# Experts in pairs: two gate-and-ups, two downs and eight transpositions in a row on TensorE

## The chip, the cores and the metric

The kernel runs on one core of a Trainium2 chip as one program. The metric is the device time of one execution in microseconds (us). The core has five engines, each with its own instruction queue: TensorE (PE, with its weight loads as PEld), VectorE (DVE), ScalarE (ACT), GpSimd (POOL) and SyncE (SP). They meet only at semaphores.
## The reference

Two transformer layers over 2048 tokens of 256 columns, float32. Layer 0 is attention and a dense feed-forward. Layer 1 is attention over groups of four and a mixture of 64 experts, of which each token takes 8. The change touches only the experts, with what the kernel does beside them:

```
_route:  scores = sigmoid(x @ gate_weight.T);  topk_idx, topk_w  (8 experts of a token)
for each expert e:
    inter = silu(x @ wg.T) * (x @ wu.T)          # 256 -> 176
    out  += (inter @ wd.T) * w_full[:, e]        # 176 -> 256
x = x + attention(xn) + moe(xn)
```

## The kernel before

The tokens' 16,384 choices are sorted by expert and cut in segments of 64 rows. Two segments, which may belong to two experts, make a block of 128 rows; there are 160 blocks (NBLK). A block goes through these steps, each named by its function:

- GpSimd gathers the block's rows from memory (`gather`, L189) into one of 8 slots of x.
- TensorE transposes them (`transpose_x`, L1832, two 128x128 transpositions into ps_xT), VectorE copies the result to xT (`copy_x`, L1719).
- TensorE multiplies with gate and up (`gate_up`, L1845). The first 64 rows use the weights of the first segment's expert where they were loaded; the other 64 use a copy of the second segment's expert, s_gu, made by ScalarE (`copy_gate_up`, L1671). So each step is two matmuls, each on 64 of the array's columns, that start together. In the trace there are four such steps per block, since each float32 product is done in two passes.
- ScalarE takes silu of the gate half (`silu`, L1653), VectorE multiplies with the up half (`gate`, L1736).
- TensorE transposes the product h (`transpose_h`, L1857, two transpositions into ps_hT), VectorE copies it to hT (`copy_h`, L1744).
- TensorE multiplies with down (`down`, L1868, again four steps of two), ScalarE scales by the router's weight (`copy_y`, L1662) and GpSimd scatters the rows to memory (`store`, L1634). The router's weight is picked by VectorE (`weigh`, L1727). The second expert's down weights are copied by ScalarE too (`copy_down`, L1676).

All 160 blocks are written out in Python: the order of each engine is the order of its code, and each step waits for semaphores that count the blocks done (`gu_ready`, `h_ready`, `hT_copied` and so on). TensorE's turn for block j is gate and up of j, down of j - 2, the register with the expert's number for j + 1 (L1837), the transpositions of x of j + 2, and those of h of j - 1. VectorE fits layer 1's attention (`attention`, L1757 to L1784) between the blocks, one step of it per block, 40 blocks to each of four batches; one exponential per batch is ScalarE's (L1691). GpSimd's turn is one gather and one scatter. SyncE loads the experts' weights, 16 experts deep (L1582 and L183 on).

After the last block TensorE multiplies the attention result with its output weights (L1897, L1904), SyncE reads the scattered rows back (L1615), and TensorE and VectorE add them up (L1930, L1547).

Of the kernel before, what the change touches and what calls it, by code (L numbers as in the profile page):

```python
# [18 lines left out]
ACT = mybir.ActivationFunctionType  # L19
AX = mybir.AxisListType  # L20

P = 128
B, T, D = 4, 512, 256
# [3 lines left out]
KD = D // P  # L27
# [22 lines left out]
HI1 = INTER1 // 2  # L50
# [1424 lines left out]
def layer1_experts(nc, t, ident, late, ring, x_sb, qkv1, seg_expert, expert_f, inv, dst, last, latest):  # L1475
# [3 lines left out]
    with ctx:  # L1479
        NS, NW, NY, NQ = ring.NS, ring.NW, SCATTERS, 4  # L1480
        LEAD, BEHIND, NF = 2, 3, 5
# [4 lines left out]
        xT = sbuf(ctx, nc, "e_xT", [P, 2, KD * P])  # L1486
# [4 lines left out]
        hT = sbuf(ctx, nc, "e_hT", [HI1, 2, 2 * P])  # L1491
# [9 lines left out]
        yT = sbuf(ctx, nc, "e_yT", [P, 2, KD, P])  # L1501
# [4 lines left out]
        ps_y = psum(ctx, nc, "e_ps_y", [P, 512])  # L1506
# [52 lines left out]
        def gate_up_copied(j):  # L1559

            return j + 1 if j < 2 else 2 * j - 1

        def down_copied(j):

            return 2 * j + 4 if j + 2 < NBLK else NBLK + j + 1
# [53 lines left out]
        def _(pool):  # L1619
# [9 lines left out]
            for j in range(NS, NS + LEAD):  # L1629
                refill(j)  # L1630
# [15 lines left out]
        def _(act):  # L1646
# [9 lines left out]
            def copy_y(j):  # L1656
                act.wait_ge(y_ready, j + 1)
                act.wait_ge(weighed, j + 1)
                if j >= NY:

                    act.wait_ge(y_out[j % NY], j // NY * 16)
                nc.scalar.activation(y[:, j % NY, :], ps_y[:, 0:D], ACT.Copy,  # L1662
                                     scale=weight[:, j % NQ:j % NQ + 1]).then_inc(y_copied, 1)
# [19 lines left out]
            for j in range(NBLK + 2):  # L1683
                n, l, k = part(j) if j < NBLK else (0, 0, None)
                if j + 2 < NBLK:
                    experts.append(expert_of(j + 2))
                if j < NBLK:
                    silu(j)
                if k == 5:
                    act.wait_ge(s_ready, n * B + B)  # L1690
                    nc.scalar.activation(e1[:, :, :], s1[:, :, :], ACT.Exp,  # L1691
                                         scale=SCALE1).then_inc(e_ready, 1)
                if j >= 2:
                    copy_y(j - 2)
                if j + 2 < NBLK:
                    copy_gate_up(j + 2, experts[j + 2])
                if j < NBLK:
                    copy_down(j, experts[j])
# [14 lines left out]
        def _(dve):  # L1713
# [3 lines left out]
            def copy_x(j):  # L1717
                dve.wait_ge(xT_ready, j + 1)
                V.tensor_copy(xT[:, j % 2, :], ps_xT[:, 0:D]).then_inc(xT_copied, 1)  # L1719
# [19 lines left out]
            def copy_h(j):  # L1739
                dve.wait_ge(hT_ready, j + 1)  # L1740
                if j >= 2:

                    dve.wait_ge(y_ready, j - 1)
                V.tensor_copy(hT[:, j % 2, :], ps_hT[0:HI1, 0:2 * P]).then_inc(hT_copied, 1)  # L1744
# [46 lines left out]

            copy_x(0)
            copy_x(1)
            weigh(0)
            for j in range(NBLK + 1):
                if j < NBLK:
                    gate(j)
                if j + 1 < NBLK:
                    weigh(j + 1)
                if j + 2 < NBLK:  # L1800
                    copy_x(j + 2)
                if j >= 1:
                    copy_h(j - 1)
                if j < NBLK:
                    attention(*part(j))
# [20 lines left out]
        def _(pe):  # L1826
            def transpose_x(j):
                pe.wait_ge(x_in[j % NS], (j // NS + 1) * 16)
                if j:
                    pe.wait_ge(xT_copied, j)  # L1830
                for k in range(KD):
                    ins = nc.tensor.transpose(ps_xT[:, k * P:(k + 1) * P],  # L1832
# [6 lines left out]
            def gate_up(j, expert):  # L1839

                pe.wait_ge(xT_copied, j + 1)
                pe.wait_ge(w_copied, gate_up_copied(j))
                for k in range(KD):
                    for r, w in ((0, w_gu[:, bass.ds(expert & (NW - 1), 1), k, :]), (1, s_gu[:, j % 2, k:k + 1, :])):
                        ins = nc.tensor.matmul(  # L1845
                            ps_gu[r * SEG:(r + 1) * SEG, j % 2, 0:2 * INTER1],
                            xT[:, j % 2, k * P + r * SEG:k * P + (r + 1) * SEG],
# [4 lines left out]
            def transpose_h(j):  # L1852
                pe.wait_ge(h_ready, j + 1)
                if j:
                    pe.wait_ge(hT_copied, j)
                for k in range(2):
                    ins = nc.tensor.transpose(ps_hT[0:HI1, k * P:(k + 1) * P],  # L1857
# [3 lines left out]
            def down(j, expert):  # L1861
                pe.wait_ge(hT_copied, j + 1)
                pe.wait_ge(w_copied, down_copied(j))
                if j:
                    pe.wait_ge(y_copied, j)
                for k in range(2):
                    for r, w in ((0, w_d[0:HI1, bass.ds(expert & (NW - 1), 1), k, :]), (1, s_d[:, j % 2, k:k + 1, :])):
                        ins = nc.tensor.matmul(  # L1868
                            ps_y[r * SEG:(r + 1) * SEG, 0:D], hT[:, j % 2, k * P + r * SEG:k * P + (r + 1) * SEG],
# [4 lines left out]
            transpose_x(0)  # L1874
            transpose_x(1)
            now, before, oldest = expert_of(0), None, None
            for j in range(NBLK + 2):
                after = None
                if j < NBLK:
                    gate_up(j, now)  # L1880
                if j >= 2:
                    down(j - 2, oldest)
                if j + 1 < NBLK:
                    after = expert_of(j + 1)
                if j + 2 < NBLK:
# [141 lines left out]
```

## Time and profile before

| | |
|---|---|
| median of 3 runs | 1199.44 us (1199.24 to 1202.48) |
| the profiled execution, its own time | 1196.38 us |
| its span (first to last instruction) | 1194.2 us |
| TensorE, matmuls | 1109.2 us busy, 93% |
| VectorE, ScalarE, GpSimd | 715.6, 658.9, 464.1 us busy |
| gate and up matmuls (L1845) | 2 x 640, 476 ns each |
| down matmuls (L1868) | 2 x 640, 380 ns each |

The experts' stage is the last big one, from about 679 us to 1138 us of the span. The busy time of TensorE counts each matmul from its start to its modelled end; matmuls overlap, so a step's real cost is the distance from its start to the next start. An average of busy time over the whole span says little about this stage; the rows below are of this stage alone.

### The profile page before, as it was taken

What the parts mean: (1) busy time and instruction counts of PE and PEld (TensorE: products, weight loads), DVE (VectorE), ACT (ScalarE), POOL (GpSimd) and SP (SyncE); (2) the same over time, 40 slices, a digit from 0 to 9 for tenths busy, and PEclk for the clock granted to TensorE, in tenths of its full rate; (3) what the DMA queues carried; (4) which work ended last, traced back from release to release, by engine and by line L of the source; (5) the groups of instructions that cost most, each with busy time, mean ns of one, the idle gap of its engine ahead of it and who ended that gap; (6) DMA issues with size and microseconds to landing.
All of it is one profiled execution on the core that took longest, in us unless ns stands there. A gap on an engine that the chain in (4) does not pass through costs nothing. (4 is left out here: it accounts for less than half of the span.)

```text
span 1194.2 us, 25537 instructions
## 1 busy us (share of the span) xinstructions
PE 1109.2 (93%) x7606; PEld 655.3 (55%) x7606; DVE 715.6 (60%) x2605; ACT 658.9 (55%) x1340; POOL 464.1 (39%) x525
## 2 busy tenths in 40 slices
PE   6679999999999999997888699999999999999985
PEld 3355666666666666654655454555455555545564
DVE  6486666565666666641259665566565656566556
ACT  4214454555555545455335567777777777777620
POOL 4332222223131000000310266777677767777500
PEclk9899999999999999999989799999999999999997
DMA  7400131113111201001104483764648436766267
GB/s 242 89 10 18 24 51 30 31 30 52 30 31 30 51 21 23 21 16 45 49 24 123 114 228 123 222 192 124 194 141 258 157 119 187 226 186 213 76 252 289
DMA packets 81682, 129.68 MB, mean 109 GB/s; under 512 B 32776, under 2 KB 53001, under 8 KB 81034
## 3 DMA queue, kind: packets, MB, share of 16 engines
q1 hardware_dynamic: 61576, 76.94, 22.7%
q0 software_dynamic: 15360, 47.21, 12.8%
q10 hardware_dynamic: 4616, 3.91, 1.1%
q8 instruction: 68, 1.11, 0.4%
q14 instruction: 62, 0.51, 0.1%
HBM read 97.57 MB, written 30.05 MB: 107 GB/s over the span
## 5 line engine op out<-in xcount | busy, mean ns | idle before, releaser
L684 DVE CUSTOM_DVE_ANT_0 a_masked<-a_ps_s,a_mask 128x512 bf16<-128x512 f32 (+3 forms) x512 | 229.9, 487 | 157.9 <-PE a_ps_s L843 154.1
L600 ACT ACTIVATE a_probs<-a_ps_e 128x512 f32<-128x512 f32 (+1 forms) x384 | 188.2, 527 | 119.9 <-PE a_ps_e L863 118.9
L1845 PE MATMUL e_ps_gu<-e_w_gu,e_xT 128*64 x640 | 226.3, 476 | 1.0 <-ACT e_s_gu L1671 1.0
L1845 PE MATMUL e_ps_gu<-e_s_gu,e_xT 128*64 128x352 f32 x640 | 226.3, 476 | 0.0
L189 POOL DMA_INDIRECT yn<-rows,inv x160 | 156.5, 978 | 138.4 <-DVE inv L1404 60.8
L1634 POOL DMA_INDIRECT y<-e_y,dst x160 | 172.3, 1077 | 59.3 <-issue 43.0
L1868 PE MATMUL e_ps_y<-e_w_d,e_hT 88*64 x640 | 165.0, 380 | 5.0 <-DVE e_hT L1744 5.0
L1868 PE MATMUL e_ps_y<-e_s_d,e_hT 88*64 88x256 f32 x640 | 165.1, 380 | 0.0
L860 PE MATMUL a_ps_e<-a_qT,a_kT 75*128 75x512 bf16 (+3 forms) x512 | 140.8, 303 | 2.1 <-ACT a_probs L600 1.8
L843 PE MATMUL a_ps_s<-a_kT,a_qT 72*128 72x512 bf16 (+3 forms) x512 | 131.3, 300 | 11.5 <-DVE a_headmax L684 11.3
L1736 DVE TENSOR_TENSOR e_h<-e_sg,e_ps_gu 128x176 f32<-128x176 f32 x160 | 53.9, 337 | 134.2 <-ACT e_sg L1653 112.0
L919 PE MATMUL a_ps_f<-a_xnT,a_w_gu 128*128 128x256 f32 x512 | 125.5, 388 | 5.6 <-DVE a_hT L709 3.2
L1868 PEld LDWEIGHTS e_ps_y<-e_w_d,e_hT 88*64 88x64 f32 x640 | 86.5, 136 | 79.2 <-issue 55.1
L1671 ACT ACTIVATE e_s_gu<-e_w_gu 128x704 f32 x160 | 124.8, 781 | 3.5 <-SPq L1582 3.5
L1662 ACT ACTIVATE e_y<-e_ps_y,e_weight 128x256 f32<-128x256 f32 x160 | 75.8, 474 | 85.7 <-PE e_ps_y L1868 85.7
L1845 PEld LDWEIGHTS e_ps_gu<-e_w_gu,e_xT 128*64 128x64 f32 x640 | 75.1, 137 | 81.0 <-issue 81.0
L863 PE MATMUL a_ps_e<-a_causal,a_identb 128*128 128x128 bf16 x512 | 112.4, 220 | 0.0
L456 POOL CAST a_m_parts<-a_negmaxT 32x128 bf16<-32x128 f32 x16 | 4.5, 281 | 275.4 <-DVE a_negmaxT L727 155.0
L919 PEld LDWEIGHTS a_ps_f<-a_xnT,a_w_gu 128*128 128x128 f32 x512 | 93.6, 192 | 22.8 <-DVE a_hT L709 10.8
L1719 DVE COPY e_xT<-e_ps_xT 128x256 f32<-128x256 f32 x160 | 67.9, 424 | 52.7 <-PE e_ps_xT L1832 52.5
L1676 ACT ACTIVATE e_s_d<-e_w_d 88x512 f32 x160 | 98.7, 617 | 0.0
L860 PEld LDWEIGHTS a_ps_e<-a_qT,a_kT 75*128 75x128 bf16 x512 | 49.2, 97 | 75.1 <-ACT a_probs L600 67.3
(243 smaller groups left out, 1893.1 us busy)
## 6 DMA issues: line engine op xcount, KB each, us to landing
e_w_gu<-e_gu SPq DMA_DIRECT2D x64, 352.0 KB
e_w_d<-e_down SPq DMA_DIRECT2D x64, 176.0 KB
a_qT<-qk_parts SPq DMA_DIRECT2D x48, 192.0 KB
e_w_gu<-y SPq DMA_DIRECT2D x12, 768.0 KB, 6.3
qk_parts<-a_stage SPq DMA_DIRECT2D x16, 256.0 KB, 2.6
e_w_gu<-y SPq DMA_DIRECT2D x4, 1024.0 KB, 7.0
qkv<-y SPq DMA_DIRECT2D x12, 256.0 KB
yn<-rows,inv POOLq DMA_INDIRECT x160
```

The source lines that it names most:

```text
L189: eng.indirect_dma_start(self.x[:, j % self.NS, :], None, t["rows"], bass.IndirectOffsetOnAxis(inv[:, j:j + 1], 0)).then_inc(self.x_in[j % ...
L600: nc.scalar.activation(probs[:, i % HKV, UCOL[u]:UCOL[u + 1]], ps_e[:, (i * 3 + u) % 2, 0:w], ACT.Exp, scale=SCALE0).then_inc(exp_done, 1)
L684: ins = V.tensor_tensor_reduce(masked[:, n % 2, c:c + w], ps_s[:, n % 2, c:c + w], mask[:, T - w:T], 1.0, -3e38, ALU.add, ALU.max, headmax ...
L843: ins = nc.tensor.matmul(ps_s[:, x % 2, c:c + (a + 1) * P], qT[0:MROW, n % NQ, g, a * P:(a + 1) * P], kT[0:MROW, b % 2, g, 0:(a + 1) * P], ...
L860: nc.tensor.matmul(ps_e[:, x % 2, c:c + T - a * P], kT[:, b % 2, g, a * P:(a + 1) * P], qT[:, n % NQ, g, a * P:T], start=True, stop=False, ...
L863: ins = nc.tensor.matmul(ps_e[:, x % 2, c:c + P], identb[:, :], causal[:, :], start=False, stop=True, skip_group_check=True)
L919: ins = nc.tensor.matmul(ps_f[:, w * HALF:(w + 1) * HALF], w_gu[:, k, w, i * P:(i + 1) * P], xnT[:, n % NX, k, :], start=(k == 0), stop=(k ...
L1634: pool.indirect_dma_start(t["y8"], bass.IndirectOffsetOnAxis(dst[:, j:j + 1], 0), y[:, j % NY, :], None).then_inc(y_out[j % NY], 16)
L1671: nc.scalar.activation(s_gu[:, j % 2].rearrange("p k i -> p (k i)"), w_gu[:, bass.ds(expert & (NW - 1), 1), :, :].rearrange("p a k i -> p ...
L1676: nc.scalar.activation(s_d[:, j % 2].rearrange("p k d -> p (k d)"), w_d[0:HI1, bass.ds(expert & (NW - 1), 1), :, :].rearrange("p a k d -> ...
L1845: ins = nc.tensor.matmul(ps_gu[r * SEG:(r + 1) * SEG, j % 2, 0:2 * INTER1], xT[:, j % 2, k * P + r * SEG:k * P + (r + 1) * SEG], w.rearran ...
L1868: ins = nc.tensor.matmul(ps_y[r * SEG:(r + 1) * SEG, 0:D], hT[:, j % 2, k * P + r * SEG:k * P + (r + 1) * SEG], w.rearrange("p a d -> p (a ...
```

## The change

TensorE takes two blocks per turn: both gate-and-ups, both downs of the pair before, the two expert numbers of the next pair, the four transpositions of x of the pair after next, and the four of h of this same pair. The transposed x of two blocks fills one bank of ps_xT and the transposed h of two blocks one bank of ps_hT, so `copy_x` and `copy_h` are done once per pair at twice the width (512 columns). ps_y has two banks, one for each block of a pair. xT and hT double, and yT, used after the stage, lies in xT. Before the first gate and up four blocks are transposed, not two. ScalarE, VectorE and GpSimd are put in the matching order; GpSimd's scatters follow four blocks behind, not three, and the router's weights have eight places, not four.

```
-            for j in range(NBLK + 2):
-                after = None
-                if j < NBLK:
-                    gate_up(j, now)
-                if j >= 2:
-                    down(j - 2, oldest)
-                if j + 1 < NBLK:
-                    after = expert_of(j + 1)
-                if j + 2 < NBLK:
-                    transpose_x(j + 2)
-                if 1 <= j <= NBLK:
-                    transpose_h(j - 1)
-                now, before, oldest = after, now, before
+            for j in range(4):
+                transpose_x(j)
+            oldest, now = None, [expert_of(j) for j in range(2)]
+            for m in range(PAIRED + 1):
+                two = (2 * m, 2 * m + 1)
+                if m < PAIRED:
+                    for j in two:
+                        gate_up(j, now[j % 2])
+                if m:
+                    for j in two:
+                        down(j - 2, oldest[j % 2])
+                if m + 1 < PAIRED:
+                    after = [expert_of(j + 2) for j in two]
+                if m + 2 < PAIRED:
+                    for j in two:
+                        transpose_x(j + 4)
+                if m < PAIRED:
+                    for j in two:
+                        transpose_h(j)
+                oldest, now = now, after
...
 (ScalarE, one pair)
+                    for j in two:
+                        silu(j)
+                        if k == 5: ... the exponential
+                        copy_gate_up(j + 2, experts[j + 2])
+                    for j in two:
+                        copy_y(j - 2)
+                    for j in two:
+                        copy_down(j, experts[j])
...
 (VectorE, one pair)
+                gate(j)
+                attention(*part(j))
+                gate(j + 1)
+                attention(*part(j + 1))
+                copy_x(m + 2)
+                copy_h(m)
+                weigh(j + 4)
+                weigh(j + 5)
...
 (GpSimd)
-            for i in range(LEAD, NBLK + BEHIND):
-                if i + NS < NBLK:
+            for i in range(NBLK + BEHIND):
+                if i + NS + LEAD < NBLK:
                     pool.wait_ge(gu_ready, i + 1)
-                    refill(i + NS)
+                    refill(i + NS + LEAD)
                 if i >= BEHIND:
                     store(i - BEHIND)
```

TensorE before, from one block's down to the next gate and up, in the middle of the stage (e_w_gu and e_w_d are the experts' weights, e_s_gu and e_s_d ScalarE's copies):

```order
L1868 MATMUL e_ps_y<-e_w_d,e_hT 64x256
L1868 MATMUL e_ps_y<-e_s_d,e_hT 64x256
L1837 TENSOR_LOAD seg_expert
L1837 ISA x2
L1832 MATMUL e_ps_xT<-ident_sb,yn 128x128 x2
L1857 MATMUL e_ps_hT<-ident_sb,e_h 88x128 x2
L1845 REGISTER_ALU
L1845 ISA
L1845 MATMUL e_ps_gu<-e_w_gu,e_xT 64x352
```

The same place in the changed kernel, where the lines of the code have moved:

```order
L1879 MATMUL e_ps_y<-e_w_d,e_hT 64x256
L1879 MATMUL e_ps_y<-e_s_d,e_hT 64x256
L1845 TENSOR_LOAD seg_expert
L1845 ISA x2
L1845 TENSOR_LOAD seg_expert
L1845 ISA x2
L1840 MATMUL e_ps_xT<-ident_sb,yn 128x128 x4
L1867 MATMUL e_ps_hT<-ident_sb,e_h 88x128 x4
L1854 REGISTER_ALU
L1854 ISA
L1854 MATMUL e_ps_gu<-e_w_gu,e_xT 64x352
```

Two register loads stand together, the transpositions are eight in a row, and this passage comes once in two blocks.

VectorE before, one block of the stage (e_h is gate's product, e_pick is weigh, e_mx and e_s are attention):

```order
L1736 TENSOR_TENSOR e_h<-e_sg,e_ps_gu 128x176
L1727 SCALAR_TENSOR_TENSOR e_pick,e_weight<-l_iota_f,expert_f,yn 128x64
L1719 COPY e_xT<-e_ps_xT 128x256
L1744 COPY e_hT<-e_ps_hT 88x256
L1764 TENSOR_REDUCE e_mx<-e_s 128x16
L1766 TENSOR_TENSOR e_s<-e_s,e_mx 128x16
```

and in the changed kernel, one pair:

```order
L1741 TENSOR_TENSOR e_h<-e_sg,e_ps_gu 128x176
L1762 TENSOR_TENSOR e_prod<-qkv 128x768
L1741 TENSOR_TENSOR e_h<-e_sg,e_ps_gu 128x176
L1765 TENSOR_REDUCE e_s<-e_prod 128x48
L1724 COPY e_xT<-e_ps_xT 128x512
L1749 COPY e_hT<-e_ps_hT 88x512
L1732 SCALAR_TENSOR_TENSOR e_pick,e_weight<-l_iota_f,expert_f,yn 128x64 x2
```

The step of attention now stands right behind each gate product, ahead of the second gate product and of both copies, and weigh stands last.

## Rows read from the trace of the kernel before

**Rows 1.** Stretches: length, busy us (instructions) per engine, clock, DMA share, GB/s
```profile
695.02:1113.00 417.98, 414.10 (x2965) 215.40 (x2966) 251.58 (x881) 305.01 (x606) 304.71 (x297) 1.00 0.58 183
```
**Rows 2.** Waits of TensorE, 692.2 to 1129: us in total, times, longest
```profile
PE e_ps_y L1868 <- DVE e_hT L1744: 3.8, 4, 1.0
```
**Rows 3.** Timeline of TensorE: start, duration, instruction, count
```profile
801.24 0.38 PE L1868 MATMUL e_ps_y<-e_w_d,e_hT 88*64 x1
...
801.55 0.44 PE L1832 MATMUL e_ps_xT<-ident_sb,yn 128*128 128x128 f32 x2
801.83 0.38 PE L1857 MATMUL e_ps_hT<-ident_sb,e_h 128*88 128x128 f32 x2
802.14 0.51 PE L1845 MATMUL e_ps_gu<-e_w_gu,e_xT 128*64 x1
...
802.49 0.46 PE L1845 MATMUL e_ps_gu<-e_w_gu,e_xT 128*64 x1
...
803.37 0.38 PE L1868 MATMUL e_ps_y<-e_w_d,e_hT 88*64 x1
...
804.02 0.38 PE L1868 MATMUL e_ps_y<-e_w_d,e_hT 88*64 x1
...
804.92 0.51 PE L1845 MATMUL e_ps_gu<-e_w_gu,e_xT 128*64 x1
```
**Rows 4.** Line L1857, 801 to 1110 us: duration ns, least/median/most
```profile
L1857 PE MATMUL e_ps_hT<-ident_sb,e_h x220: 272/273/273, 801.8 to 1109.6; 128*88 128x128 f32 x110
```
**Rows 5.** Timeline of ScalarE and VectorE, the same block, [idle before <-releaser]
```profile
802.04 0.78 ACT L1671 ACTIVATE e_s_gu<-e_w_gu 128x704 f32 x1
...
802.37 0.41 DVE L1744 COPY e_hT<-e_ps_hT 88x256 f32<-88x256 f32 x1
...
803.59 0.32 ACT L1653 ACTIVATE e_sg<-e_ps_gu 128x176 f32<-128x176 f32 x1 [0.25 <-PE e_ps_gu L1845]
...
804.00 0.34 DVE L1736 TENSOR_TENSOR e_h<-e_sg,e_ps_gu 128x176 f32<-128x176 f32 x1 [0.89 <-DVE e_s L1760]
```
**Rows 6.** Line L1784, attention's longest step: duration ns, least/median/most
```profile
L1784 DVE TENSOR_REDUCE qkv<-e_prod x16: 405/856/1960, 730.2 to 1118.7; 128x256 f32<-128x256 f32 x4, 128x256 f32<-128x512 f32 x4, 128x256 f32<-128x768 f32 x4, 128x256 f32<-128x1024 f32 x4
```
**Rows 7.** Timeline at the first of the four exponentials
```profile
719.10 1.28 ACT L1691 ACT_TABLE_LOAD   x1
...
720.39 0.34 ACT L1691 ACTIVATE e_e<-e_s 128x160 f32<-128x160 f32 x1
...
725.30 0.42 PE L1868 MATMUL e_ps_y<-e_w_d,e_hT 88*64 x1 [0.95 <-DVE e_hT L1744]
```
**Rows 8.** TensorE's sequencer (PEldq), lines L1837 and L1830: durations ns, first start
```profile
L1837 PEldq TENSOR_LOAD <-seg_expert x109: 298/303/572, 803.1 to 1107.9; - x109
...
L1830 PEldq EVENT_SEMAPHORE  x109: 51/51/51, 803.7 to 1108.6; - x109
```
**Rows 9.** GpSimd's groups, 692 to 1100: busy us, mean ns | idle before
```profile
L1634 POOL DMA_INDIRECT y<-e_y,dst x144 | 155.6, 1080 | 43.9 <-issue 39.0 <-ACT e_y L1662 2.1 <-DVE e_pick L1727 1.2
L189 POOL DMA_INDIRECT yn<-rows,inv x145 | 141.8, 978 | 70.3 <-issue 46.2 <-PE e_ps_gu L1845 16.1 <-PE e_ps_xT L1832 6.4
```
**Rows 10.** Timeline at the start of the stage
```profile
679.74 0.94 POOL L189 DMA_INDIRECT yn<-rows,inv  x1 [2.96 <-POOLq L1158]
...
680.99 0.95 POOL L189 DMA_INDIRECT yn<-rows,inv  x1 [0.30 <-issue]
...
684.95 0.69 PE L1832 MATMUL e_ps_xT<-ident_sb,yn 128*128 128x128 f32 x2 [0.54 <-DMA yn<-rows,inv]
...
689.16 0.80 PE L1845 MATMUL e_ps_gu<-e_w_gu,e_xT 128*64 x1
```
**Rows 11.** Stretches again, the first two blocks
```profile
681.70:689.50 7.80, 7.16 (x24) 2.80 (x26) 2.16 (x10) 3.25 (x7) 5.92 (x7) 0.50 1.15 229
```
**Rows 12.** Timeline at the end of the stage
```profile
1129.28 0.51 PE L1845 MATMUL e_ps_gu<-e_w_gu,e_xT 128*64 x1
...
1138.95 0.97 POOL L1634 DMA_INDIRECT y<-e_y,dst  x1 [1.07 <-ACT e_y L1662]
```

More of the change, by code:

```diff
@@ L1559, in gate_up_copied @@
         def gate_up_copied(j):
-            return j + 1 if j < 2 else 2 * j - 1
+            return j + 1 if j < 2 else 4 * (j // 2) - 2 + j % 2 + 1
         def down_copied(j):
-            return 2 * j + 4 if j + 2 < NBLK else NBLK + j + 1
+            return 4 * (j // 2) + j % 2 + (5 if j + 2 < NBLK else 3)
         def part(j):
@@ L1635, in store @@
                                         y[:, j % NY, :], None).then_inc(y_out[j % NY], 16)
-            for i in range(LEAD, NBLK + BEHIND):
-                if i + NS < NBLK:
+            for j in range(NS, NS + LEAD):
+                refill(j)
+            for i in range(NBLK + BEHIND):
+                if i + NS + LEAD < NBLK:
                     pool.wait_ge(gu_ready, i + 1)
-                    refill(i + NS)
+                    refill(i + NS + LEAD)
                 if i >= BEHIND:
@@ L1790, in add_attention @@
                 V.tensor_tensor(x_sb[:, i, :], x_sb[:, i, :], ps_out[q % 2][:, 0:D], ALU.add).then_inc(o_added, 1)
[L1792 to L1797, printed above, removed]
-                if j + 1 < NBLK:
[L1799 to L1805, printed above, removed]
+            for m in range(2):
+                copy_x(m)
+                for j in (2 * m, 2 * m + 1):
+                    weigh(j)
+            for m in range(PAIRED):
+                j = 2 * m
+                gate(j)
[5 more added lines that the diff above has]
+                copy_h(m)
+                if m + 2 < PAIRED:
+                    weigh(j + 4)
+                    weigh(j + 5)
                 if j == FIRST_ROWS_AT:
@@ L1828, in transpose_x @@
                 pe.wait_ge(x_in[j % NS], (j // NS + 1) * 16)
-                if j:
-                    pe.wait_ge(xT_copied, j)
+                if j >= 2 and j % 2 == 0:
+                    pe.wait_ge(xT_copied, j // 2)
                 for k in range(KD):
-                    ins = nc.tensor.transpose(ps_xT[:, k * P:(k + 1) * P],
+                    c = j % 2 * KD * P + k * P
+                    ins = nc.tensor.transpose(ps_xT[:, c:c + P],
                                               x[:, j % NS, k * P:(k + 1) * P], ident[:, :])
@@ L1853, in transpose_h @@
                 pe.wait_ge(h_ready, j + 1)
-                if j:
-                    pe.wait_ge(hT_copied, j)
+                if j >= 2 and j % 2 == 0:
+                    pe.wait_ge(hT_copied, j // 2)
                 for k in range(2):
-                    ins = nc.tensor.transpose(ps_hT[0:HI1, k * P:(k + 1) * P],
+                    c = j % 2 * 2 * P + k * P
+                    ins = nc.tensor.transpose(ps_hT[0:HI1, c:c + P],
                                               h[:, j % 2, k * HI1:(k + 1) * HI1], ident[:, :])
```

82 lines of the change are left out of this document (39 added, 43 removed).

## The prediction

> **What bounds the kernel now.** I read the table of stretches first. In the experts' stage, about 455 of the 1194 us, TensorE is busy 414.1 of 418.0 us, VectorE 251.6, ScalarE 305.0 and GpSimd 304.7, and the granted clock is 1.00 [rows 1]. The waits come next: over the same stage TensorE waits for another engine only four times, 3.8 us in all, each time for the copy of hT [rows 2]. So the stage lasts as long as TensorE's own row of instructions, and one block of it is the unit of the sum.
>
> The timeline of one block shows where its time goes [rows 3]. Each line is one of two matmuls that start together on the two halves of the array's columns. From one gate-and-up start to the next it is 804.92 - 802.14 = 2.78 us. Inside a group the starts come evenly: gate and up every (803.37 - 802.49)/3 = 0.293 us, down every (804.02 - 803.37)/3 = 0.217 us. A transposition takes 0.109: the two of hT begin at 801.83, the group ends at 802.21 and one lasts 0.273 [rows 3, 4], so the second began at 801.94. Between the groups more goes by:
> - last down to first transposition: 801.55 - 801.24 = 0.31, which is 0.10 over the step of 0.217
> - the first transposition: two steps take 801.83 - 801.55 = 0.28, which is 0.06 over 2 x 0.109
> - last transposition to gate and up: 802.14 - 801.83 = 0.31, which is 0.09 over 2 x 0.109
> - the first gate-and-up step: 802.49 - 802.14 = 0.35, which is 0.06 over 0.293.
> From gate and up to down nothing extra shows. So 0.31 us of each block's 2.78 are the two changes between 64-column matmuls and full-width transpositions.
>
> **The change part by part.** The matmuls, their shapes and their number stay. TensorE's order becomes two gate-and-ups, two downs, four transpositions of x, four of h, so both changes come once per pair.
>
> *Switching.* 78 pairs lie between the third block and the last pair: 78 x 0.31 = 24.2 us saved. A pair takes 2 x 2.78 - 0.31 = 5.26 us. Bounds: if the 0.10 at the entry belongs to something that stays with each block, 78 x 0.21 = 16.4; above 0.31 no row shows anything to gain.
>
> *Transposition of h now follows its own pair.* Before, it waited a whole block; now only the two downs and x's four transpositions cover it. Within a pair from t = 0 at its first gate and up: silu can start 803.59 - 802.14 = 1.45 later, the gate product 804.00 - 802.14 = 1.86 later [rows 5]. The second block's are 1.18 later, at 2.63 and 3.04, h ready at about 3.4. ScalarE does silu (0.32), the copy of the next gate-and-up weights (0.78 from 1.77 to 2.55) and is free for the second silu at 2.63. The transposition that needs the second h comes at 8 x 0.293 + 8 x 0.217 + 0.16 + 6 x 0.109 = 4.9. VectorE can push the second gate product out by the attention step of the even block, 0.41 to 1.96 us by the longest of its steps [rows 6]: at most 2.2 + 1.96 + 0.34 = 4.5. That is still in time. Cost 0; the cover is 1.5 us in most pairs and 0.4 in the worst.
>
> *The copies are twice as wide.* The trace has no 512-wide copy. hT's copy of 256 columns takes 0.41 [rows 5]. The bounds are 0.41 (the width is free) and 0.82 (two copies); I take 0.69, a fixed part of some 0.13 paid once. x's copy starts at 5.0, when its transpositions are through, and hT's ends at 6.4 (5.8 and 6.6 at the bounds). The next pair's down is due at 5.26 + 2.35 = 7.6. Cover 1.2 us, nothing either way. Four pairs hold the longest steps of attention: with 1.96 in the odd block alone the copies still end at 6.8, with as much in the even one at 8.7, 1.1 late. Bound 4 us, taken 0, since the even block's step is a shorter one.
>
> *Exponential.* Its four stalls stay. Two table loads of 1.28 and the exponential (0.34) stand between two silus [rows 7]. Before, that makes the down wait for hT 0.95 [rows 7]. Now the second silu of that pair comes at 1.77 + 1.28 + 0.25 + 0.78 + 1.28 = about 5.4, h at 6.1 against 4.9 due: 1.2 each. Against 0.95 and the slower restart behind it (some 0.25) that is even; bounds -1 to +2 us for the four.
>
> *GpSimd.* One gather and one scatter per block: 0.978 + 1.080 busy and twice the least gap of 0.30 [rows 9] make 2.66 per block, 5.32 a pair, against TensorE's 5.26 and 5.33 with the four stalls spread over the pairs. It is on the edge. But a gather has three pairs (over 15 us less its landing) until TensorE needs it, and a scatter eight slots. In 146 blocks it would fall behind by 146 x 0.03 = 4 us at most, and the last ten blocks need no gather. Cost 0.
>
> *Start.* Now four gathered blocks must be there before the first gate and up; only two were. The third's gather is issued at 679.74 and holds TensorE until 684.95; the fourth's at 680.99 [rows 10], so by the same 5.2 us it lands at 686.2. The clock is at 0.50 (1.2 GHz) in that stretch [rows 11], where everything takes double: 8 gate-and-up steps 4.7 us. First gate and up 686.7, second h ready about 692.5, third block's gate and up 691.9 to 693.3, by whether the clock has risen meanwhile. Before it was at 689.16 [rows 10]. Cost 2.7 to 4.1; I take 3.4. The Trainium skill (TensorE: Matmul & The Clock Gate, Part 4: PE-mode transpose) says that transpositions do not count as TensorE activity for the clock. By it the later end would be right, 0.7 us more; no row here separates it.
>
> *Tail.* From the second-last block's gate and up to the last scatter: 1138.95 - 1129.28 = 9.67 us [rows 12]. Now, by the same steps: gate and up 2.4, down 1.7, four transpositions 0.6, latency and copy 1.0, down to the first y 1.1, ScalarE's copy 0.5, two scatters: the last begins at 8.8. Gain 0.9. The output stage behind it is untouched.
>
> Sum: -24.2 + 3.4 - 0.9 = -21.7 us. The profiled execution took 1196.38 us, so it would be 1174.7. The median of the runs shown is 1199.44, 3.1 above it; the forecast in the terms of those runs is 1177.7.
>
> **The rivals.**
> A, the forecast: the switches go. 1177.7.
>
> B, GpSimd or late gathers take part of it. For it: it has 5.32 of work in 5.33 us, and single scatters take longer. Against it: the slack above. To cost anything its pace must exceed 2.67 + 13/146 = 2.76 us per block; it would then be near 1186 (half of the switches' gain lost, up to 1190).
>
> C, the sequencer is the bound: slower. The place is the two register loads behind two downs. When the load came at 803.1 [rows 8] the array stood at the last gate-and-up step, so all of one down, 8 matmuls and 8 weight loads, had been dispatched. That is all the row shows; two downs behind one gate and up want 48. If only 16 fit, the load starts when the second down starts, 4 x 0.217 = 0.87 before the transpositions, and two loads take 1.2: at least 0.33 late per pair, some 0.4 with what follows them. 79 x 0.4 = 31.6, so 1199.4 + 31.6 - 21.7 = 1209.3. It decides when less than about 28 instructions fit; at 0.27 us per pair the gain is gone.
> The Trainium skill (TensorE: Matmul & The Clock Gate, the table at its head) gives a depth of 64 for the queue. By that figure C would not occur; the rows here only show 16.
>
> D, the 0.31 us is not switching but goes with each block (its waits and register work). Against it: no extra shows between gate and up and down, where the same kind of waits stand. Then only start and tail count: 1199.4 + 2.5 = 1201.9.
>
> E, the clock falls. The eight transpositions and the stall at the exponential leave some 2.4 us with no matmul, four times. At the start a stretch of 7.8 us runs at 0.50 [rows 11] and costs half of it; four of those are 15.6, giving 1193.3. Against it: before, the stalls are followed by no drop (1.00) [rows 1].
> The rule quoted above, that transpositions are no activity, speaks for E; the stage of rows 1 has a switch to them in every block and shows full clock.
>
> **Chances.** A 0.80, B 0.08, C 0.05, D 0.03, E 0.04. A, B and E are faster: 0.91 with the doubt that some of B may end within 0.3%. C and a part of what I haven't thought of are slower: 0.06. D with the rest: 0.03. The bound of 0.3% (3.6 us) is about what a measurement of this kernel can tell from no change. The range: down from 1177.7, the exponential's 1 us, the better start (0.7) and the runs' own spread (3 us) give 1173; up, 16.4 instead of 24.2 gives 1185.5, with the later start and 2 us at the exponential 1188.
>
> **What would show it.** In the profile after, pairs of blocks 5.26 us apart; inside one, 0.31 us between down and transpositions and between these and gate and up once per pair, and the second gate and up right behind the first at 0.29. TensorE's waits list four for h of some 1.2 us and nothing else of size. The third gate and up starts near 692.6. Copies of 512 take about 0.69 us. GpSimd's gaps shrink to 0.30. C would show as 0.7 us instead of 0.31 between down and transpositions, with nobody named for it; B as waits of TensorE for gathered rows or of ScalarE's y copy for scatters; E as a clock below 1.00 between 700 and 1100. I am wrong if a pair takes more than 5.5 us.

## The result and the profile after

| | before | after |
|---|---|---|
| median of the first comparison, us | 1200.96 (4 runs, 1199.24 to 1204.78) | 1183.06 (4 runs, 1178.64 to 1184.52) |
| profiled execution, own time, us | 1196.38 | 1184.52 |
| its span, us | 1194.2 | 1182.7 |

The ratio after over before is 0.9844, with a 95% interval of 0.9813 to 0.9876: 17.9 us faster at the medians, where 21.7 were forecast (1177.7, range 1173 to 1188). On two other chips the sign was the other one, 1.010 and 1.008. The experiments below had to explain that as well. Ratios, here and below, are of fast runs alone; the only slow runs are three of the kernel before on the second chip.

Cut at four events that both traces have, the program reads so, in us:

| part | before | after | difference | forecast |
|---|---|---|---|---|
| span's start to the first transposition of x | 679.14 | 687.59 | +8.45 | 0 |
| to the third block's gate and up | 10.02 | 15.58 | +5.56 | +3.4 |
| to the second-last block's gate and up | 440.12 | 415.46 | -24.66 | -24.2 |
| to the last scatter | 9.67 | 8.90 | -0.77 | -0.9 |

The first row is code that the change doesn't touch. It differs between executions of one kernel too (684.52 and 685.76 in two more profiles of the changed kernel, 682.56 in one more of before, 683.77 in a kernel that is the one before up to there and ran beside the first experiments), and the 679.14 is the earliest of all fourteen profiles. The three rows of the stage sum to -19.9.

**The middle.** The timeline of TensorE in the profile after, one border between pairs; the lines answer to [rows 3]:
```profile
803.18 0.38 PE L1879 MATMUL e_ps_y<-e_w_d,e_hT 88*64 x1
...
803.49 0.66 PE L1840 MATMUL e_ps_xT<-ident_sb,yn 128*128 128x128 f32 x4
803.98 0.60 PE L1867 MATMUL e_ps_hT<-ident_sb,e_h 128*88 128x128 f32 x4
...
806.93 0.38 PE L1879 MATMUL e_ps_y<-e_w_d,e_hT 88*64 x1
...
808.76 0.66 PE L1840 MATMUL e_ps_xT<-ident_sb,yn 128*128 128x128 f32 x4
```
From one group of transpositions to the next it is 808.76 - 803.49 = 5.27 us, where 5.26 were forecast and two blocks took 5.57. The 0.31 between the last down and the first transposition is there as before, once per pair.

The waits of TensorE, 680 to 1120 us, as [rows 2] shows them of before (us in total, times, longest):
```profile
PE e_ps_xT L1840 <- DMA yn<-rows,inv: 6.4, 2, 4.8
PE e_ps_xT L1840 <- PEq L1158: 4.3, 1, 4.3
PE e_ps_hT L1867 <- DVE e_h L1741: 4.1, 4, 1.0
PE e_ps_gu L1854 <- DVE e_xT L1724: 1.1, 1, 1.1
```
Four waits of 1 us for h, at the four exponentials; all the rest stands at the start of the stage. The stretch of the middle part, whose fields are those of [rows 1], the width of x's copy and GpSimd's groups, which answer to [rows 9]:
```profile
703.17:1118.63 415.46, 411.33 (x3118) 236.29 (x3117) 254.77 (x770) 317.34 (x637) 306.85 (x304) 1.00 0.60 187
```
```profile
L1724 DVE COPY e_xT<-e_ps_xT x78: 669/692/693, 703.1 to 1113.5; 128x512 f32<-128x512 f32 x78
```
```profile
L189 POOL DMA_INDIRECT yn<-rows,inv x148 | 150.4, 1016 | 55.8 <-issue 32.5 <-DVE e_pick L1732 11.3 <-PE e_ps_gu L1854 11.0
L1633 POOL DMA_INDIRECT y<-e_y,dst x144 | 145.7, 1012 | 45.5 <-issue 25.0 <-ACT e_y L1663 7.9 <-PE e_ps_gu L1854 7.3
```
The clock is 1.00 (2.4 GHz). The 512-wide copy takes 0.69 us. GpSimd has 101 us of gaps beside 296 of work, so it doesn't set the pace.

**The start.** Timeline, and under it TensorE's sequencer at the lines that read the experts' numbers (durations in ns, first and last start):
```profile
689.43 0.98 POOL L189 DMA_INDIRECT yn<-rows,inv  x1 [0.30 <-issue]
...
695.41 0.69 PE L1840 MATMUL e_ps_xT<-ident_sb,yn 128*128 128x128 f32 x2 [1.54 <-DMA yn<-rows,inv]
...
696.14 0.69 DVE L1724 COPY e_xT<-e_ps_xT 128x512 f32<-128x512 f32 x1 [6.53 <-PE e_ps_xT L1840]
...
697.24 0.84 PE L1854 MATMUL e_ps_gu<-e_w_gu,e_xT 128*64 x1 [1.14 <-DVE e_xT L1724]
```
```profile
L1845 PEldq TENSOR_LOAD <-seg_expert x4: 303/310/487, 695.4 to 698.5; - x4
L1845 PEldq FUSED_REGOPS  x4: 151/154/165, 696.0 to 698.8; - x4
```
The fourth block's transposition begins at 695.41, when its gather has landed, and the first register load begins at the same 695.4. The sequencer had not gone past the transposition that waited. The loads that the prediction counted as free so stand in the open here, beside the copy of x.

### The profile page after: what moved, and what is told of

It reads as the page before. It is cut to its first block and busy times, and to the rows that moved or that the text cites. A ratio compares the mean times of both kernels' runs of the same rounds, so it can differ in the third digit from the quotient of the medians.

```text
span 1182.7 us, 25082 instructions
## 1 busy us (share of the span) xinstructions
PE 1087.1 (92%) x7605; PEld 667.5 (56%) x7606; DVE 704.8 (60%) x2445; ACT 655.8 (55%) x1340; POOL 459.1 (39%) x525
## 5 line engine op out<-in xcount | busy, mean ns | idle before, releaser
L1854 PE MATMUL e_ps_gu<-e_w_gu,e_xT 128*64 x640 | 208.6, 469 | 1.1 <-DVE e_xT L1724 1.1
L189 POOL DMA_INDIRECT yn<-rows,inv x160 | 162.1, 1013 | 122.3 <-DVE inv L1404 60.5
L1854 PE MATMUL e_ps_gu<-e_s_gu,e_xT 128*64 128x352 f32 x640 | 208.6, 469 | 0.0
L1633 POOL DMA_INDIRECT y<-e_y,dst x160 | 161.3, 1008 | 60.5 <-issue 28.9
L1879 PE MATMUL e_ps_y<-e_w_d,e_hT 88*64 x640 | 151.4, 379 | 0.9 <-DVE e_hT L1749 0.9
L1879 PE MATMUL e_ps_y<-e_s_d,e_hT 88*64 88x256 f32 x640 | 151.4, 379 | 0.0
L1854 PEld LDWEIGHTS e_ps_gu<-e_w_gu,e_xT 128*64 128x64 f32 x640 | 81.7, 137 | 90.6 <-issue 90.6
L1724 DVE COPY e_xT<-e_ps_xT 128x512 f32<-128x512 f32 x80 | 55.2, 690 | 92.7 <-PE e_ps_xT L1840 92.6
L1654 ACT ACTIVATE e_sg<-e_ps_gu 128x176 f32<-128x176 f32 x160 | 50.7, 317 | 85.1 <-PE e_ps_gu L1854 79.8
L1677 ACT ACTIVATE e_s_d<-e_w_d 88x512 f32 x160 | 90.9, 617 | 0.0
```

What stands on the lines that cost most here:

```text
L189: eng.indirect_dma_start(self.x[:, j % self.NS, :], None, t["rows"], bass.IndirectOffsetOnAxis(inv[:, j:j + 1], 0)).then_inc(self.x_in[j % ...
L1633: pool.indirect_dma_start(t["y8"], bass.IndirectOffsetOnAxis(dst[:, j:j + 1], 0), y[:, j % NY, :], None).then_inc(y_out[j % NY], 16)
L1677: nc.scalar.activation(s_d[:, j % 2].rearrange("p k d -> p (k d)"), w_d[0:HI1, bass.ds(expert & (NW - 1), 1), :, :].rearrange("p a k d -> ...
L1854: ins = nc.tensor.matmul(ps_gu[r * SEG:(r + 1) * SEG, j % 2, 0:2 * INTER1], xT[:, j // 2 % 2, j % 2, k * P + r * SEG:k * P + (r + 1) * SEG ...
L1879: ins = nc.tensor.matmul(ps_y[r * SEG:(r + 1) * SEG, j % 2, 0:D], hT[:, j // 2 % 2, j % 2, k * P + r * SEG:k * P + (r + 1) * SEG], w.rearr ...
```

## The experiments

Twelve kernels ran, on three chips. The kernel before took 1203.7 us (median of 9) beside the first four, 1291.2 (13) beside the next four and 1293.6 (18) beside the last four. Which chip gave the first comparison isn't on record; its times are those of the first of these three, and "the first chip" means both.

### One more change of width in every block

The kernel before, x's transpositions moved between gate and up and down:
```
                    gate_up(j, now)
+                if j + 2 < NBLK:
+                    transpose_x(j + 2)
                 if j >= 2:
                     down(j - 2, oldest)
...
-                if j + 2 < NBLK:
-                    transpose_x(j + 2)
```

> The kernel before with one move on TensorE: the transpositions of x stand between gate and up and down, those of h stay behind down. The same instructions, but four changes between 64-column matmuls and full-width transpositions per block instead of two. Theory A (the change of kind costs 0.31 us per pair of changes): a block goes from 2.79 to 3.10 us, 158 blocks give +49 us, about 1250 against 1201. Theory D (the extra goes with the block, with its waits and register work): 2.79 us and no difference, 1201.

It took 1240.64 us (2 runs), 1.033 of before (1.025 to 1.041). Timeline of TensorE:
```profile
801.70 0.51 PE L1845 MATMUL e_ps_gu<-e_w_gu,e_xT 128*64 x1
...
803.04 0.44 PE L1832 MATMUL e_ps_xT<-ident_sb,yn 128*128 128x128 f32 x2
803.41 0.43 PE L1868 MATMUL e_ps_y<-e_w_d,e_hT 88*64 x1
...
803.67 0.38 PE L1868 MATMUL e_ps_y<-e_w_d,e_hT 88*64 x1
...
804.42 0.42 PE L1857 MATMUL e_ps_hT<-ident_sb,e_h 128*88 128x128 f32 x2
804.77 0.51 PE L1845 MATMUL e_ps_gu<-e_w_gu,e_xT 128*64 x1
```
A block takes 3.07 us instead of 2.79, so a way there and back costs 0.28 at this place. The middle part takes 479.77 us, 39.65 more: that is 156 x 0.28 = 43.7, less what the waits for hT lose (one of 0.6 us is left of the 3.8). Between gate and up and down, where no extra time stood before, the change of width now costs what it costs elsewhere. Rival D is out: it doesn't go with the block.

### The same in the pair

The changed kernel, x's four transpositions between the gate-and-ups and the downs:
```
+                if m + 2 < PAIRED:
+                    for j in two:
+                        transpose_x(j + 4)
                 if m:
                     for j in two:
                         down(j - 2, oldest[j % 2])
...
-                if m + 2 < PAIRED:
-                    for j in two:
-                        transpose_x(j + 4)
```

> The changed kernel with the four transpositions of x moved ahead of the two downs: four changes of kind per pair instead of two, everything else in pairs. Theory A: a pair goes from 5.27 to 5.58 us, 78 pairs give back 24 us, about 1207 against 1183 (the time before, plus the longer start). Theory D, and any theory in which the gain comes from the wider copies, the two banks of y or the fewer semaphores: the pair stays at 5.27, 1183.

1201.63 us (8 runs), ratio 1.0001 (0.9975 to 1.0027), a pair 5.55. The middle part takes 435.97 us: one added switch per pair, with the pairing itself kept, gives 20.5 of the 24.66 us back, and the longer start, which this kernel has too (16.31 us), takes the rest. With as many switches as before, the pairing alone makes the middle part 4.15 us shorter (440.12 - 435.97), of which 0.73 has only moved to the start (the last whole pair has no x to transpose and takes 4.82); all else of the gain is the switch.

### Width or transposing mode

The next two replace the transpositions with ordinary matmuls against the identity, first at full width:
```
-                    ins = nc.tensor.transpose(ps_xT[:, c:c + P],
-                                              x[:, j % NS, k * P:(k + 1) * P], ident[:, :])
+                    ins = nc.tensor.matmul(ps_xT[:, c:c + P],
+                                           x[:, j % NS, k * P:(k + 1) * P], ident[:, :],
+                                           start=True, stop=True, skip_group_check=True)
```

> The changed kernel with each transposition done as an ordinary float32 matmul with the identity, still on the full width (128 columns for x, 88 for h). That takes two passes of 128 rows, by the 0.293 us of 352 columns 0.107 each, so eight of them take 1.71 us instead of 0.87 and the pair 6.1 us. If the extra at the changes belongs to the width (theory W), the 0.10 and 0.06 at the entry and the 0.09 and 0.06 at the exit stay: pair 6.1 us, about 1249. If it belongs to the transposing mode (theory M), they go: pair 5.8 us, about 1225.

1257.03 us (1 run), a pair 6.21, near the 6.1 of theory W. The last down starts at 802.59 and x at 802.91, 0.32 as ever; the first gate-and-up step still takes 0.34. With no transposing instruction left, the cost stays.

Then on halves of the array's columns, x in 64 and 64, h in 64 and 24:
```
+                    for a, b in ((0, SEG), (SEG, HI1)):
+                        ins = nc.tensor.matmul(ps_hT[a:b, c:c + P],
+                                               h[:, j % 2, k * HI1 + a:k * HI1 + b], ident[:, :], ...)
```

> The changed kernel with each transposition done as two ordinary matmuls with the identity that stand side by side on the array's column halves (64 and 64 columns for x, 64 and 24 for h), as gate, up and down do. Two side by side start together, so they cost 1.71 us a pair as in the full-width run. Theory W (width): no change of width is left and the 0.31 us go: pair 5.8 us, about 1225, 24 us less than the full-width run. Theory M (mode): both runs alike, 5.8 us. If neither, both at 6.1 us.

1376.05 us (1 run), a pair 7.74, far over both expectations. Timeline of TensorE:
```profile
801.74 0.38 PE L1883 MATMUL e_ps_y<-e_w_d,e_hT 88*64 x1
...
801.95 1.05 PE L1841 MATMUL e_ps_xT<-ident_sb,yn 128*64 128x128 f32 x16
802.83 2.79 PE L1870 MATMUL e_ps_hT<-ident_sb,e_h 128*64 128x128 f32 x16
805.54 0.51 PE L1856 MATMUL e_ps_gu<-e_w_gu,e_xT 128*64 x1
```
At the entry the theory of the width holds: 801.95 - 801.74 = 0.21, no extra. But h takes 2.71 us where x takes 0.88 for as many matmuls. Its halves are the only ones of unequal width. If each change between 64 and 24 costs as one between 64 and full, that is where it comes from; the next kernel tests this.

### Every matmul 64 columns wide

The same, h's second half reading on to 64 columns (what lies past its 24 is computed and not used):
```
-                    for a, b in ((0, SEG), (SEG, HI1)):
+                    for a, b in ((0, SEG), (SEG, P)):
```

> The kernel with the transpositions as ordinary matmuls on halves of the array's columns, where now h's second half is 64 columns wide like the first (it reads on into the next columns, and those results are not used), so that every matmul of the stage has 64 columns. Theory W (a change of the tile's width costs, and nothing else): h's group takes as long as x's, 0.88 us instead of 2.7, no extra time stands at any border of groups, and a pair is 8 x 0.293 + 8 x 0.217 + 2 x 0.88 = 5.84 us, the time 1183 + 78 x 0.57 = 1227. If the 0.17 at the way back to gate and up belongs to something else, such as x's copy or the first gate-and-up step itself, a pair is 6.0 and the time 1240. If h's 2.7 us came from something other than its unequal halves, a pair stays at 7.7 and the time at 1376.

It ran on the second chip, 1359.5 us (1 run) where the changed kernel took 1303.1, so its time says little; its pairs without a wait do. Timeline of TensorE:
```profile
706.15 0.38 PE L1884 MATMUL e_ps_y<-e_w_d,e_hT 88*64 x1
...
706.36 1.04 PE L1842 MATMUL e_ps_xT<-ident_sb,yn 128*64 128x128 f32 x16
707.24 1.04 PE L1871 MATMUL e_ps_hT<-ident_sb,e_h 128*64 128x128 f32 x16
708.11 0.46 PE L1857 MATMUL e_ps_gu<-e_w_gu,e_xT 128*64 x1
...
708.41 0.46 PE L1857 MATMUL e_ps_gu<-e_w_gu,e_xT 128*64 x1
```
0.21 into x, 0.88 for x, 0.87 for h, and a first gate-and-up step of 0.30 instead of 0.35: no extra at any border. The five quickest whole pairs take 5.84 or 5.85 us, where 5.84 were expected. The cost is the change of the tile's width. It isn't a better kernel: as ordinary matmuls on halves, the transpositions take 1.75 us a pair (708.11 - 706.36) where the changed kernel takes 1.02.

### The changed kernel again, on another chip

> The changed kernel once more, with no edit, as a base for the others. If the late beginning of the experts' stage in its first profile (first transposition of x at 687.59 against 679.14 us) is chance of an execution, since the code ahead of it is the same, it will be elsewhere here, while the time from the first transposition of x to the third block's gate and up comes again as 15.6 us, the middle part as 415.5 and a pair as 5.27. If the start's 15.6 hangs on that late beginning, it will be other than 15.6 when the beginning is. Time 1183.

1303.08 us (10 runs) against 1291.21, ratio 1.0099 (1.0063 to 1.0135): here the change makes the kernel slower. The program up to this stage takes as long as on the first chip. In the experts' stage the shortest whole pair is still 5.27, but the median is 6.34 and the longest 12.3. One of the long ones, in the timeline of the three engines:
```profile
886.87 0.66 PE L1840 MATMUL e_ps_xT<-ident_sb,yn 128*128 128x128 f32 x4
887.37 0.60 PE L1867 MATMUL e_ps_hT<-ident_sb,e_h 128*88 128x128 f32 x4
...
893.15 0.69 DVE L1724 COPY e_xT<-e_ps_xT 128x512 f32<-128x512 f32 x1 [7.20 <-remote]
893.94 0.69 DVE L1749 COPY e_hT<-e_ps_hT 88x512 f32<-88x512 f32 x1
...
894.77 0.68 PE L1879 MATMUL e_ps_y<-e_w_d,e_hT 88*64 x1 [4.28 <-DVE e_hT L1749]
```
The transpositions of x start at 886.87 and last 0.66, yet VectorE, which waits for nothing but their signal, copies at 893.15, 5.6 us after their end. "remote" means that the profile finds no releaser. In the first chip's profile this copy follows at once, at 889.79 behind transpositions of 889.0. The gathers aren't slower there: from issue to the last landing they take a median of 2.9 us on the other two chips, and 3.3 (before) and 3.5 (changed) on the first. Waits of this kind for TensorE appear in the experts' stage of every profile of the second and the third chip (of the changed kernel here, 22 before copies of x and 44 before ScalarE's silu and copies of y), and in none of the first. What holds TensorE's signals back on these chips stays open.

The start came again, with 15.91 us (15.58 in the first profile).

### Registers first

```
+            oldest, now = None, [expert_of(j) for j in range(2)]
             for j in range(4):
                 transpose_x(j)
-            oldest, now = None, [expert_of(j) for j in range(2)]
```

> The changed kernel, where TensorE reads the first two experts' numbers ahead of the four first transpositions instead of behind them. Theory S (the start's excess is TensorE's own program order: its sequencer stands at the transposition that waits for the fourth gather, and the two loads of 0.6 us each come after it): the time from the first transposition of x to the third block's gate and up falls from 15.58 to about 14.3 us, and the first gate and up follows the last transposition by under 1 us instead of 1.8. Theory G (only the gathers are late, the loads are hidden): it stays at 15.6. The time itself, 1182 against 1183, can't tell them apart; the trace does.

The fourth gather came very late in this execution (7.75 us of wait), so the length of the start, 18.59, can't be used. What stands behind the last transposition can:
```profile
697.23 0.69 PE L1840 MATMUL e_ps_xT<-ident_sb,yn 128*128 128x128 f32 x2 [7.75 <-DMA yn<-rows,inv]
697.85 0.85 PE L1854 MATMUL e_ps_gu<-e_w_gu,e_xT 128*64 x1
```
0.62 us instead of 1.83 (697.24 - 695.41 in the profile after) and 1.84 (694.78 - 692.94 in the kernel run beside it). Theory S holds: 1.2 us of the start were the loads behind the waiting transposition. But they haven't become free. The first transposition, in the changed kernel beside it and then here:
```profile
684.52 0.72 PE L1840 MATMUL e_ps_xT<-ident_sb,yn 128*128 128x128 f32 x4 [4.29 <-PEq L1158]
```
```profile
685.43 1.11 PE L1840 MATMUL e_ps_xT<-ident_sb,yn 128*128 128x128 f32 x4 [5.85 <-issue]
```
TensorE now stands 5.85 us before it instead of 4.29, with the first load at 683.9: the loads cost 1.5 us there. In this kernel that is hidden, since the third and the fourth gather come later anyway. The times (1305.22, ratio 1.0104, 1.0019 to 1.0188) don't tell it.

### Two blocks ahead instead of four

```
-            for j in range(4):
+            for j in range(2):
                 transpose_x(j)
...
                         gate_up(j, now[j % 2])
+                if m < 2:
+                    for j in two:
+                        transpose_x(j + 2)
```

> The changed kernel, where only two blocks of x are transposed ahead of the first gate and up (registers read first), the next two behind the first pair's gate and up, and the two after them behind the second pair's; VectorE's copies and its weighing of the rows follow. If the start's cost is the wait for the third and the fourth gather, the time from the first transposition of x to the third block's gate and up comes back from 15.58 to 9.5 to 10.5 us (before the change 10.02), and the kernel gains about 5 us: 1178. If the gathers are not what holds it, but the pairing itself (two gate and ups at half clock, then h), it stays above 14 and the time at 1183.

The first gate and up came 2.09 us after the first transposition (10.26 in the changed kernel beside it), the third 12.04 (15.91). So the gathers do hold the start. The 9.5 to 10.5 wasn't reached, since TensorE waited 3.73 us for the second h. And the time from the first transposition flatters this kernel: with the loads first, TensorE stood 5.79 us before that transposition instead of 4.29. Counted from TensorE's last matmul ahead of it, the third gate and up comes after 17.8 us instead of 20.2, a gain of 2.4 and not 3.9. 1305.23 us, ratio 1.0121 (1.0042 to 1.0200) against 1.0099: on that chip no gain in time.

### Before, once more, beside the changed kernel

> The kernel before, once more with a profile. Two questions. First, where the experts' stage begins: if the late first transposition of x in the changed kernel's profiles (683.8 to 688.5 us in nine of them, 679.14 in the one of before) is chance, it lies between 683 and 689 here too; if it belongs to the change, at 679 again. Second, if this chip is one that stretches the experts' stage, as the last one did (pairs of 5.27 us with a median of 6.3), whether the kernel before loses as much per block: by the times there (1291 against 1204) it would lose some 87 us, the changed kernel 120.

> The changed kernel once more, as the base for the next two and because the last call's chip turned the sign (1.010 of before). If that was the chip, this one gives 0.980 to 0.988 of before again, with pairs of 5.27 us. If the chip stretches the stage again, it is 1.00 to 1.01 of before.

A third chip, of the second one's kind. Before: 1293.64 us (18 runs). Changed: 1304.00 (6), ratio 1.0077 (1.0048 to 1.0106). The first transposition of x lies at 682.56 in before, where its first profile had 679.14 and the kernel with one more change of width, which is the same up to there, 683.77. The eleven profiles of the changed kernel and its variants have 683.3 to 688.5. So a large part of the +8.45 was chance; whether some of it belongs to the change stays open. The stretch from the third block's gate and up to the second-last one's, before and then changed (busy us of TensorE, its weight loads, VectorE, ScalarE, GpSimd, then the clock):
```profile
692.48:1219.38 526.90, 456.89 (x3121) 224.76 (x3121) 266.62 (x931) 313.39 (x638) 308.75 (x306) 0.99 0.48 149
```
```profile
701.67:1240.55 538.88, 460.93 (x3118) 249.35 (x3117) 253.93 (x770) 309.40 (x637) 307.48 (x304) 0.93 0.46 144
```
With the same two stretches of the first chip beside them (before: 440.12 us, TensorE busy 436.24), the 12.0 us that the change loses here fall into three terms:
- The switches, as there: 411.33 - 436.24 = -24.9.
- The idle time: 538.88 - 460.93 = 77.95 against 526.90 - 456.89 = 70.0, while on the first chip it was 4 in both: +8.
- The clock: TensorE's busy time is 460.93 - 411.33 = 49.6 over that of the first chip in the changed kernel, 456.89 - 436.24 = 20.7 in before: +29. The granted clock is 0.93 against 0.99, and 0.06 of some 460 us is 28, so nearly all of this difference is the clock. The other 20 us are in both kernels; the 0.99 of before accounts for some 5 of them, and what makes the rest isn't known.

The waits of TensorE give a reason. Before, 692 to 1240 us, and then changed, the largest rows:
```profile
PE e_ps_y L1868 <- DVE e_hT L1744: 51.7, 47, 2.6
```
```profile
PE e_ps_y L1879 <- DVE e_hT L1749: 41.3, 24, 6.2
PE e_ps_hT L1867 <- DVE e_h L1741: 23.4, 18, 3.2
```
Somewhat more waiting (with the smaller rows of the stage some 70 us before and 76 after), and above all in other pieces: before 47 of 1.1 us, none over 2.6, and after 42 of 1.5 us, up to 6.2. Behind the longest one the clock has fallen; the steps of the changed kernel, and then the granted clock (the figure before the last two) of the pair ahead of it and of the pair with it:
```profile
1219.49 0.68 PE L1879 MATMUL e_ps_y<-e_w_d,e_hT 88*64 x1 [6.19 <-DVE e_hT L1749]
...
1220.40 0.63 PE L1879 MATMUL e_ps_y<-e_w_d,e_hT 88*64 x1
1220.82 0.63 PE L1879 MATMUL e_ps_y<-e_w_d,e_hT 88*64 x1
```
```profile
1205.45:1210.72 5.27, 5.27 (x42) 3.04 (x41) 2.81 (x9) 3.40 (x7) 3.98 (x5) 1.00 0.36 112
1210.72:1225.01 14.29, 8.10 (x42) 4.31 (x41) 3.70 (x12) 5.87 (x12) 6.84 (x7) 0.78 0.22 70
```
Steps of 0.42 us instead of 0.217, so the lower level (1.2 GHz). That the long waits cause the loss is argued from such places; no run took them away.

### The exponential later, and with the early start

```
-                        n, l, k = part(j)
-                        if k == 5:
+                        n, l, k = part(2 * m)
+                        if j % 2 and k == 5:
```

> The changed kernel, where ScalarE computes the exponential of attention behind the second silu of a pair instead of behind the first. My reading: the four waits of TensorE for h (4.1 us, 1.0 each) come from the two table loads and the exponential between the two silus of a pair; now both silus are done before them, the wait for h goes, and what is late instead is the copy of the down weights and of the next gate-and-up weights, by about 0.5 us: 4 x 0.5 = 2 us are gained, 1181 against 1183. Rival: the 2.9 us of ScalarE simply move to the next thing that TensorE waits for, and as much is lost in another row (four waits of 1 us or more at w_gu or y): 1183 to 1185.

1299.82 us (9 runs), ratio 1.0055 (1.0030 to 1.0081), against 1.0077 for the changed kernel: in the direction of the first reading, with intervals that overlap. Its middle part took 534.44 us against 538.88. In the waits a new row has come, 16.1 us in 6 times for the copy of the down weights, as both theories had it, but there the late signals are in it too. Not settled.

> The changed kernel with both edits: only two blocks of x ahead of the first gate and up, and the exponential behind the second silu. If the start's cost was the two extra gathers and the register loads, the time from the first transposition of x to the third block's gate and up is 10 to 12 us instead of 15.6, and with the 2 us of the exponential the kernel gains 5 to 7 us: 1177, 0.979 of before. If the early start only moves the wait (the second pair's h stands behind transpositions that wait for gathers, as 3.7 us of a wait for h did in the last call), 1182.

1304.35 us (6 runs), ratio 1.0085 (1.0057 to 1.0113). The start took 12.00 us instead of 15.91, with 3.86 us of wait for the second h; as above, 1.5 of the gain only moved ahead of the first transposition (5.83 us of idle time instead of 4.35). Behind it stands the same late signal, here at ScalarE's silu, 2 us after the gate and up was through:
```profile
692.74 0.32 ACT L1654 ACTIVATE e_sg<-e_ps_gu 128x176 f32<-128x176 f32 x1 [3.12 <-remote]
```
The middle took 544.49 instead of 538.88. No faster version was shown; on a chip like the first neither edit was run.

## Why the prediction was right, and where not

- **Switching, -24.2.** Right: the middle part gave -24.66, a pair 5.27. About 0.45 of it has only moved: the start now transposes four blocks of x ahead of the first gate and up, and the last whole pair none (4.82 us). The added switches (0.28 each, in single blocks and in pairs) and the kernel with none confirm the price and the cause.
- **h behind its own pair, the copies, GpSimd: nothing.** Right on the first chip: four waits of 1.0 for h, copies of 0.69, gaps on GpSimd. The cover of 0.4 to 1.5 us was all that was left, and the prediction treated it as enough without asking what it costs if TensorE's signals come later. On two other chips they do, and TensorE waits for them (in the profile of the third chip 24 times for hT, 41.3 us, and 18 times for h, 23.4 us); this is the step that fails there.
- **Exponential, even.** Right: 4.1 us of waits where [rows 2] have 3.8.
- **Registers, free.** Right in the pairs: the loads of the pair of 804.5 us come at 806.4, when one gate-and-up step and both downs, some 36 instructions, were still to do; rival C is out. The Trainium skill (TensorE: Matmul & The Clock Gate, the table at its head) gives the queue a depth of 64; the trace agrees as far as those 36. Wrong at the start, where they follow a transposition that waits for a gather.
- **Start, +3.4.** The direction was right, the size was off: +5.56. The mis-sized term is the first gate and up, put at 686.7, that is 7.6 us after the first transposition; it came 9.65 after it. 1.2 of the 2.1 missing are the register loads behind the waiting transposition. 0.8 is the later gather: issued at 689.43, in the array at 695.41, 6.0 where 5.2 were taken. From the first gate and up to the third block's it took 5.93 us (703.17 - 697.24), the middle of the prediction's bracket of 5.2 to 6.6: the steps took 0.59 us, at the lower clock, until the last one, and full speed was back before the transpositions behind them (four starts in 0.49 us, 701.89 to 702.38). Whether transpositions have a part in when the clock rises, no run here tells.
- **Tail, -0.9.** -0.77.
- **Rival E, the clock falls.** False on the first chip: 1.00 with eight transpositions and a stall of 1 us together. On the others it is the larger part of the loss, most likely by a way that the prediction didn't have: long waits for late signals, not the exponential.
- **The sum.** -19.9 in the stage against -21.7; the medians gave -17.9 with an interval from -15 to -22. Two profiled executions alone would have said -11.5, because of the 8.45 us in code that is the same.

## What to carry to other kernels

Look for extra time at the borders between groups of TensorE instructions. Where tiles of different width meet, put those of one width together, and test by adding a switch, which is easier to read than taking one away. Then ask what the longer groups do to the cover of every result that is waited for: the same change, with covers of 0.4 to 1.5 us, was a gain on one chip and a loss on two others, where the waits grew longer and the clock fell behind the longest. Look for register loads that stand behind an instruction of the same engine that waits for a transfer, and measure from a point ahead of every place that they could move to: here 1.2 us behind the transposition became 1.5 us ahead of the first one.

## What the runs showed of the hardware

- A change of tile width costs 0.28 to 0.31 us there and back, between 64 columns and full width, in fp32, whether the wide ones are transpositions or ordinary matmuls. Halves of 64 and 24 columns side by side pay it inside the group: 16 such matmuls took 2.71 us, 16 of 64 and 64 took 0.87.
- A transposition of 128x128 in fp32 takes 0.109 to 0.12 us, the same as an ordinary matmul about 0.25 (x's four from 802.91 to 803.90, with the entry).
- TensorE's sequencer ran some 36 instructions ahead of the array (the load at 806.4), but not past a transposition whose gather was outstanding: the loads behind it began with it, at 695.4 and, on the second chip, at 692.9.
- Two of three chips held TensorE's signals back, by 5.6 us in the case shown, in this stage and not ahead of it, and took some 7.5% longer for the kernel before.
